# Causal masks by matmul: each identity half streams only its own 64 columns

## The reference

```python
scores = jnp.einsum('bshd,bthd->bhst', q, k) / jnp.sqrt(jnp.asarray(D, x.dtype))
causal = jnp.triu(jnp.ones((S, S), dtype=bool), k=1)
scores = jnp.where(causal[None, None], -jnp.inf, scores)
attn = jax.nn.softmax(scores, axis=-1)
```

## Time and profile before

| what | us |
|---|---|
| median of 3 runs | 652.57 |
| lowest and highest | 652.37, 657.2 |
| the profiled execution | 650.28 |
| its span, first to last instruction | 648.5 |
| TensorE busy in the span | 621.4 (96%) |
| VectorE, ScalarE, GpSimd busy | 437.5, 306.0, 321.6 |

### The profile page before, as it was taken

The page is one execution under the profiler, slowest core; times in us unless marked ns, Lnnn a source line. Parts: engine busy times, 40 slices in busy tenths (PEclk is TensorE's granted clock), DMA queues, the critical chain, the costliest instruction groups (busy, mean ns, idle before and its releaser), DMA issues.

```text
span 648.5 us, 17789 instructions
## 1 busy us (share of the span) xinstructions
PE 621.4 (96%) x4929; PEld 368.7 (57%) x4929; DVE 437.5 (67%) x1364; ACT 306.0 (47%) x798; POOL 321.6 (50%) x340
## 2 busy tenths in 40 slices
PE   7999999999998999999999999999999999999997
PEld 3644455655554555555555555555554666666654
DVE  6768687568665766676665565445446788889865
ACT  3643121024444444444444444445454776777752
POOL 4000000268637766568656776664301766666662
PEclk9999999999999999999999999999999999999999
DMA  9510011138979769995899878995416777877432
GB/s 294 175 37 2 0 34 34 55 85 271 274 243 283 242 190 289 350 304 171 246 310 301 272 230 261 329 271 133 99 50 199 236 218 216 239 218 219 124 105 74
DMA packets 78167, 124.52 MB, mean 192 GB/s; under 512 B 11113, under 2 KB 52618, under 8 KB 78090
## 3 DMA queue, kind: packets, MB, share of 16 engines
q1 hardware_dynamic: 43098, 60.18, 30.4%
q0 software_dynamic: 15872, 46.16, 24.2%
q10 hardware_dynamic: 19120, 17.18, 7.8%
HBM read 85.73 MB, written 37.75 MB: 190 GB/s over the span
## 4 chain that ended last, share of the span: by engine, by line
PE 83%; DVE 5%; DMA 4%; issue 3%; ACT 2%; POOL 2%; DVEq 1%; ACTq 0%; SPq 0%; POOLq 0%
PE pair L1211 23%; PE pair L1238 14%; PE pair L1181 6%; PE pair L1168 5%; PE pair L1116 4%; PE bank L1323 4%; PE bank L1222 3%; PE bank L1195 3%; PE bank L1355 2%; PE pair L1078 2%; PE pair L1278 2%; PE pair L1297 2%; DMA lower<-xn_rows,idx_all 2%; PE pair L1286 2%; DVE negm L980 2%
## 5 line engine op out<-in xcount | busy, mean ns | idle before, releaser
L453 POOL DMA_INDIRECT lower<-xn_rows,idx_all x128 | 139.3, 1089 | 215.0 <-DVE idx_all L953 107.8
L1211 PE MATMUL pair<-space,work 128*64 (+1 forms) x768 | 165.6, 463 | 7.0 <-DVE wqkv_sb L927 3.7
L1238 PE MATMUL pair<-lower,work 88*64 x512 | 122.1, 380 | 1.8 <-ACT lower L614 1.4
L1211 PEld LDWEIGHTS pair<-space,work 128*64 128x64 f32 x768 | 66.8, 137 | 77.7 <-issue 67.2
L869 DVE TENSOR_TENSOR work<-work,pair 128x176 f32<-128x176 f32 x128 | 42.8, 337 | 90.9 <-ACT work L608 90.4
L1238 PEld LDWEIGHTS pair<-lower,work 88*64 88x64 f32 x512 | 69.3, 137 | 50.8 <-issue 20.9
L1211 PE MATMUL pair<-wqkv_sb,work 128*64 128x352 f32 x256 | 89.4, 472 | 0.0
L614 ACT ACTIVATE lower<-pair 128x256 f32<-128x256 f32 x128 | 49.1, 383 | 77.8 <-PE pair L1238 77.8
L518 POOL DMA_INDIRECT wqkv_sb<-y_rows,slot_i x48 | 46.9, 977 | 60.9 <-DVE negm L980 34.0
L980 DVE TENSOR_REDUCE negm<-pair 128x2 f32<-128x256 f32 (+1 forms) x128 | 64.9, 551 | 11.4 <-PE pair L1286 9.9
L659 ACT ACTIVATE pT<-pair 128x768 f32<-128x768 f32 x64 | 51.9, 811 | 42.6 <-PE pair L1309 41.3
(11 more groups left out here) (202 smaller groups left out, 1168.6 us busy)
## 6 DMA issues: line engine op xcount, KB each, us to landing
space<-wgu SPq DMA_DIRECT2D x66, 352.0 KB
y_rows<-lower ACTq DMA_DIRECT2D x128, 128.0 KB
qk_all<-qk_rows SPq DMA_DIRECT2D x64, 256.0 KB, 4.2
lower<-wdn SPq DMA_DIRECT2D x64, 176.0 KB
qk_rows<-qk_all POOLq DMA_DIRECT2D x32, 256.0 KB
qk_rows<-space POOLq DMA_DIRECT2D x16, 256.0 KB
xn_rows<-qk_all SPq DMA_DIRECT2D x16, 128.0 KB, 1.8
lower<-xn_rows,idx_all POOLq DMA_INDIRECT x128
```

Source lines behind the costliest of these rows:

```text
L453: po.indirect_dma_start(xg[:, r % XB, :], None, xn_rows[:, :], bass.IndirectOffsetOnAxis(idx_all[:, r:r + 1], 0)).then_inc(xg_in[r % XB], 16)
L1211: last = pe.matmul(pair[u % 2][strip, 0:2 * F], xgT[u][:, c, strip], n, start=c == 0, stop=c == EC - 1, skip_group_check=True)
L1238: last = pe.matmul(pair[u % 2][strip, 512:512 + E], hT[:, u % 2, c, strip], n, start=c == 0, stop=c == 1, skip_group_check=True)
```

## The change

Each half now streams only the 64 columns in which its own half of the identity is not zero, and writes only those. So the identity has to be what streams. In `turned_masks` it already was. In `score_masks` mask and identity change places, and the mask that stays in the array has to be transposed: `below_b`, new, which is minus 1e30 where the row is greater than the column. VectorE works it out from `tri_f` in place (an add of `id_f` and a scalar instruction, after the copy to `tri_b`, each waiting for the one before it), and `half_masks` makes its bf16 halves with four more copies, in the room of the first four parts of `run_b`, for which ScalarE waits until the counts have been used. `exp_table` reads another tile, as `run_b` is overwritten. The matmuls are as many as before; each streams 2 x 64 columns in place of 2 x 128.

```diff
+        below_b = run_b[:].rearrange("p t e -> p (t e)")[:, 0:2 * P].rearrange("p (h q) -> p h q", h=2)
...
-                    act.activation(col[:, 0:1], run_b[:, 0, 0:1], ACT.Exp)
+                    act.activation(col[:, 0:1], rstd[:, 0:1], ACT.Exp)
...
                 act.wait_ge(id_in, 16)
-                for to, src in ((id_b, id_f), (mask_b, mask_f)):
+                act.wait_ge(consts_b, 1)
+                act.wait_ge(counted, 1)
+                for to, src in ((id_b, id_f), (mask_b, mask_f), (below_b, tri_f)):
...
-            dve.tensor_copy(tri_b[:], tri_f[:])
+            link(dve.tensor_copy(tri_b[:], tri_f[:]))
+            link(dve.tensor_tensor(tri_f[:], tri_f[:], id_f[:], ALU.add))
+            dve.tensor_scalar(tri_f[:], tri_f[:], -1.0, -MASKED, ALU.add, ALU.mult)
...
                 for h in range(2):
+                    part = slice(h * 64, (h + 1) * 64)
                     for j in range(2):
-                        o = score_room[m % 2][:, 512 * j:512 * (j + 1)].rearrange("p (s k) -> p s k", s=2)[:, :, 0:P]
-                        pe.matmul(o, id_b[own[j], h], mask_b[own[j], h].unsqueeze(1).to_broadcast([64, 2, P]),
+                        o = score_room[m % 2][:, 512 * j:512 * (j + 1)].rearrange("p (s k) -> p s k", s=2)[:, :, part]
+                        pe.matmul(o, below_b[own[j], h], id_b[own[j], h, part].unsqueeze(1).to_broadcast([64, 2, 64]),
                                   start=h == 0, stop=False, skip_group_check=True)
...
                 for h in range(2):
+                    part = slice(h * 64, (h + 1) * 64)
                     for j in range(2):
-                        o = pair[1][:, 512 * j:512 * (j + 1)].rearrange("p (s k) -> p s k", s=2)[:, :, 0:P]
-                        pe.matmul(o, mask_b[own[j], h], id_b[own[j], h].unsqueeze(1).to_broadcast([64, 2, P]),
+                        o = pair[1][:, 512 * j:512 * (j + 1)].rearrange("p (s k) -> p s k", s=2)[:, :, part]
+                        pe.matmul(o, mask_b[own[j], h], id_b[own[j], h, part].unsqueeze(1).to_broadcast([64, 2, 64]),
                                   start=h == 0, stop=False, skip_group_check=True)
```

## The result

The changed kernel took 649.06 us in the median of 20 runs (645.27 to 652.41), the kernel before 652.82 in 20 runs (650.28 to 657.2). The ratio is 0.9934, with a 95% interval of 0.9915 to 0.9953. The forecast of 648.4 and the direction were right: 4.2 us or 0.64% of 652.57 was forecast, 0.66% was measured.

What follows compares the result with a forecast made beforehand. TensorE, 83% of the chain of waits, was taken to bound the kernel, with VectorE holding residual to `m_transpose`. 3.4 + 0.4 + 0.1 + 0.4 - 0.1 = 4.2 us gave 648.4 us, range 646.2 to 651.8 (8 in 10).

Steps and rivals of the forecast that it cites:

- The step: Score-mask groups: spacing from first to second pair falls from 0.12 us, saving 0.054 to 0.063, taken as 0.057.
- The second pair is hidden, the first counts: Mask groups in steady slots: second pair's 0.107 us stream hides behind a 0.11 weight load, so halving it gains nothing.
- The rival in which both count: Mask groups: both pairs' streams save, 0.114 a group, 8.1 us in all, giving 644.4 us; chance 0.14.
- Ten groups count, slot 2 does not: `m_transpose` to `o_project`: ten of 12 groups save, 0.57 us a batch, 3.4 over six; slot 2 waits for ScalarE.
- The rival in which ScalarE binds slots 0 and 4: Steady batches: exponentials and copies set the pace there too, six groups of twelve count, 2.7 us, 649.9; chance 0.08.
- No floor: Pair spacing: forecast follows the columns; the rival floor has step 0.095, saving 0.025, sum 1.8, 650.8 us; chance 0.12.
- Below zero: Slots before the first batch: both pairs count in four rounds of 2.26 us, 0.107 each, 0.4 us gained.
- last slots: Slots 57 to 63: only turned masks remain, each on the loop with the exponential; 7 x 0.057 = 0.4 us gained.
- first batch: Slots 0 to 7: exponentials, then `halves` and gathers set the pace; 0 to 0.8 us possible, 0.1 taken.
- The set-up: Before the projections: two VectorE instructions add 0.4 to 0.65 us, 0.38 covered, cost taken as 0.1; ScalarE's copies covered.
- VectorE doesn't bind: Steady batches: VectorE's 1.46 us idle before the residual is more than twice the 0.57 gain; was to fall to about 0.9.
- the rival on the slow side: Last slots: smaller masks let TensorE's clock fall to 1.2 GHz, about +12 us, giving 660; chance 0.05.

Runs made afterwards that it cites:

- the raw copy put first: Changed kernel with ScalarE emptying the values before the ring copy in every odd slot; 646.85 us in one profiled execution, attention 151.75.
- the gathers' six slots of lead: Changed kernel with raw copy first, sums moved, `halves` before normalisation, and expert-row gathers allowed six slots earlier; 642.57 us, ratio 0.9819 to the kernel before.
- second profile: Changed kernel unaltered, timed again beside the kernel before with each run's granted clock; 649.81 us against 653.85, ratio 0.9942, attention 151.82.
- the score masks alone: Changed kernel with the turned masks' matmuls put back as before, so only plain score masks stream 64 columns; 650.28 us, attention 153.86.
- the first pair alone: Changed kernel, but only the first pair of each group streams 64 columns twice, the second 128 twice; 645.73 us, attention 152.04.
- half of the columns: Changed kernel streaming 2 x 32 columns per mask matmul in place of 2 x 64, half the mask left out; 645.38 us, attention 150.20.
- the set-up alone: Changed kernel's tables and copies with the mask matmuls of the kernel before; 652.96 us against 654.08, ratio 0.999, attention 155.95.
- both orders: Changed kernel with raw copy first in odd slots, slot 5 and 6 sums moved, `halves` ahead of normalisation; 643.62 us, ratio 0.9838 to the kernel before.

## Why the prediction was right, point by point

- **The step** of a pair: 0.057 was taken as the saving, 0.054 came (0.120 to 0.066). The row of the routing, a step of 0.057 for 128 columns and so a saving of 0.063, was a little too good; "keeping the 0.013 above the stream" was the true reading, as the run with 64 columns shows. This is the only size off in the main term: six stretches gave 6 x 0.53 = 3.2, forecast 3.4.
- **The second pair is hidden, the first counts:** shown by the two runs with one pair each, 12.48 and 11.94. The prediction had read the cover for the score masks only (the loads of L1286) and carried it over to the turned masks; 12.48 was measured with both kinds, so it holds there too. The rival in which both count (11.3 by its price) is out.
- **Ten groups count, slot 2 does not:** 0.53 is ten steps of 0.054, to the rounding, and either kind alone gives half of it. The rival in which ScalarE binds slots 0 and 4 would have given 12.1. That slot 2 hangs on ScalarE was shown by the raw copy put first.
- **No floor:** shown by the steps of 0.066 and 0.039. The Trainium skill (TensorE: Matmul & The Clock Gate, Back-to-back issue gap) has about 81 ns for a 128-column matmul in a stream with weight loads; these pairs differ from it, each standing in two halves of the array, but the measurement decides, 66 ns here and 57 ns in the routing.
- **Below zero** 0.37, and 0.1 ahead of the first maximum (from the first mask to it 1.69 before, 1.58 after), forecast 0.4; the **last slots** 0.37, forecast 0.4. The **first batch** gave 0.04, forecast 0.1: its `m_transpose` waits for gathers that wait for the first maxima, and the gathers' six slots of lead took 1.1 from it together with the other edits.
- **The set-up** costs nothing; 0.1 was taken. The step that failed is "the exponential on ScalarE waits for it; its table load starts at 26.88" as a cover of 0.38: the table load isn't behind the subtraction at all but behind ScalarE's instruction before it, in the trace of before too, and its 1.28 cover the delay on their own.
- **One sign was wrong.** VectorE's wait before the residual was to fall from 1.46 to about 0.9 and fell to 1.40. That wait is `o_project` itself, which got no shorter; the room came out of VectorE's smaller waits between slots: all its idle time in a batch fell from 2.17 to 1.84. The argument for "VectorE doesn't bind" thus rested on the wrong row, though it held. TensorE's wait before `m_transpose` grew as forecast, from 0.48 to 0.69, by the four groups of slots 6 and 7.
- **The clock** kept 1.00 in the last slots, so the rival on the slow side is out there. It looked at the last slots only; the half-rate stretch that did come lay in the expert loop, and with the waits around it made up 3.2 us of the 4.6 by which the attention started later in the profiled execution.

In sum: 3.2 + 0.37 + 0.04 + 0.37 = 4.0 in the attention, and 3.8 and 4.0 between the medians. The sum in the attention is shown part by part. That the medians agree with it to 0.2 is closer than their intervals, of about 1.2 us either way and more, can vouch for.

## What to carry to other kernels

Ask of each matmul what else runs under it: here a stream of 0.107 us beside a weight load of 0.11 was free, and only the streams that spaced the next start were worth cutting. Before an engine's cut is counted, mark the stretches that another engine holds (here VectorE around `halves`, ScalarE in slot 2); three reorderings and an earlier gather on those other engines gave another 5.8 us in the attention (151.82 to 146.05), and 7.2 between the medians of the runs (649.81 to 642.57), more than the halved streams gave. Where single executions scatter by 1%, compare the stage by its own first and last instruction.

## What the runs showed of the hardware that was not expected

The granted clock fell to half for a few us at a place that no change touched: between 200 and 210 us, in the expert loop, it averaged 0.66 in the changed kernel, in its second profile and with the score masks alone, 0.83 in six other experiments, and 1.00 in the profiles of before, of the first pair alone, of half of the columns and of the set-up alone. TensorE waits for gathered rows there in every one of the 13 profiles, but the length of the longest wait doesn't tell the two apart: 1.36 to 2.97 us where the clock fell, 0.69 to 1.73 where it didn't. One profile (both orders) has a fall at 150.8 too. In the attention a fall followed a wait of 1.07 ahead of an `m_transpose` once, and a wait of 1.06 at the same place brought none. What decides it was not settled.

Such stretches are not bound to the change: in the 29 runs of the kernel before that were timed in the rounds of the experiments, 21 had a mean clock below 1.000, as had 23 of 27 runs of the changed kernel. But the mean was 0.9953 in the 27 and 0.9972 in the 29, and 7 of the 27 were at 0.992 or under, none of the 29 and one of the 12 with the set-up alone. So the changed kernel probably loses the clock a little more often or for longer; by which mechanism, no run shows. Its cost isn't shown either: the four runs of the changed kernel at 1.000 have a median of 646.5 and the eight of the kernel before 652.9, more apart than the 4.0 of the attention, but they come from different rounds.

A table load on ScalarE started before the input of its activation was there (26.65 against 26.85). And the step from one pair of matmuls in two halves of the array to the next was the columns at 2.4 GHz and 0.013 us, for 256, 128 and 64 columns.
